# First attention of a two-layer transformer on one Trainium2 core: values and sums in one PSUM block of strips, the sums over four steps

## The reference, cut to what matters

```python
Q1, Q2 = Q[..., :dh], Q[..., dh:]                 # dh = 16
K1, K2 = K[..., :dh], K[..., dh:]
A1 = where(causal, Q1 @ K1.T * scaling, -inf)     # 2048 x 2048, and A2 likewise
attn = softmax(A1, -1) - lam * softmax(A2, -1)
O = attn @ V                                      # V: 2048 x 32
```

## Time and profile before

| | us |
|---|---|
| median of 3 runs | 4359.77 |
| lowest and highest run | 4359.03, 4366.46 |
| the profiled execution: its time | 4362.48 |
| the profiled execution: its span in the trace | 4360.6 |
| TensorE busy | 3700.6 (85% of the span) |
| VectorE busy | 2467.0 (57%) |
| ScalarE busy | 1754.4 (40%) |
| GpSimd busy | 1706.6 (39%) |

### The profile page before, as it was taken

How to read it: one execution, slowest core, us unless ns; L and a number is a source line. 1 busy time by engine, 2 the same in 40 slices (tenths; PEclk the granted TensorE clock), 3 DMA queues, 4 the chain that set the end, 5 groups by cost and what they waited for, 6 DMA issues and landing times. The chain is left out here.

```text
span 4360.6 us, 69689 instructions
## 1 busy us (share of the span) xinstructions
PE 3700.6 (85%) x21166; PEld 1647.8 (38%) x21231; DVE 2467.0 (57%) x4628; ACT 1754.4 (40%) x3522; POOL 1706.6 (39%) x1117
## 2 busy tenths in 40 slices
PE   6869999999999999999999996753899678896794
PEld 3322333232323232323233323642455445555462
DVE  4456766575757576767676753767211276666102
ACT  2324665666656566666666663110122141111110
POOL 1313555555555555555555554400344231110203
PEclk9978999999999999999999997855899899996897
DMA  4431111111111111111111103210443200001332
GB/s 156 154 120 33 34 37 33 34 35 35 35 35 35 35 35 35 35 36 34 38 33 38 31 9 96 82 40 0 121 91 76 45 24 4 0 0 39 111 111 87
DMA packets 202326, 224.92 MB, mean 52 GB/s; under 512 B 86673, under 2 KB 162706, under 8 KB 195858
## 3 DMA queue, kind: packets, MB, share of 16 engines
q1 hardware_dynamic: 186642, 195.39, 15.3%
q0 software_dynamic: 15360, 25.44, 3.1%
HBM read 139.12 MB, written 80.87 MB: 50 GB/s over the span
## 5 line engine op out<-in xcount | busy, mean ns | idle before, releaser
L638 POOL TENSOR_TENSOR attention_probs<-attention_probs 128x1024 f32<-128x1024 f32 (+2 forms) x640 | 1228.1, 1921 | 1160.2 <-PE attention_ps_o L791 1160.1
L708 DVE TENSOR_REDUCE attention_chunk_max<-attention_ps_m 128x1 f32<-128x512 f32 (+3 forms) x2560 | 1394.2, 604 | 457.4 <-PE attention_ps_m L823 280.6
L683 ACT ACTIVATE attention_probs<-attention_ps_s 128x512 f32<-128x512 f32 (+3 forms) x2560 | 1199.5, 532 | 826.9 <-PE attention_ps_s L772 459.7
L768 PE MATMUL attention_ps_s<-attention_q_stack,attention_k_stack 99*128 99x512 bf16 (+3 forms) x2560 | 821.6, 354 | 91.1 <-ACT attention_probs L683 70.1
L820 PE MATMUL attention_ps_m<-attention_k_stack,attention_q_stack 96*128 96x512 bf16 (+3 forms) x2560 | 772.5, 357 | 48.7 <-DMA attention_v_head<-v_rows 34.5
L791 PE MATMUL attention_ps_o<-attention_probs,attention_v_head 128*32 128x512 f32 (+3 forms) x5120 | 647.4, 558 | 8.6 <-issue 5.0
L768 PEld LDWEIGHTS attention_ps_s<-attention_q_stack,attention_k_stack 99*128 99x128 bf16 x2560 | 234.0, 98 | 668.4 <-ACT attention_probs L683 466.0
L820 PEld LDWEIGHTS attention_ps_m<-attention_k_stack,attention_q_stack 96*128 96x128 bf16 x2560 | 224.9, 97 | 628.7 <-DVE attention_chunk_max L708 490.2
L809 PE MATMUL attention_ps_l<-attention_probs,consts 128*32 128x512 f32 (+1 forms) x2560 | 352.6, 580 | 9.7 <-POOL attention_probs L638 1.0
L734 DVE TENSOR_TENSOR attention_out_sb<-attention_even_sb,attention_odd_sb 64x512 f32<-64x512 f32 x128 | 115.0, 898 | 296.8 <-ACT attention_even_sb L656 290.9
L823 PE MATMUL attention_ps_m<-mask_q_bf,ident_bf 128*128 128x128 bf16 x1024 | 225.5, 223 | 0.0
(11 more groups left out here) (283 smaller groups left out, 4108.8 us busy)
## 6 DMA issues: line engine op xcount, KB each, us to landing
qk_parts<-project_parts SPq DMA_DIRECT2D x64, 384.0 KB, 3.0
heads_out<-attention_out_sb SPq DMA_DIRECT2D x128, 128.0 KB, 2.3
out_heads<-heads_out SPq DMA_DIRECT2D x8, 2048.0 KB, 8.2
experts_w<-in_f_w SPq DMA_DIRECT2D x16, 1024.0 KB, 8.3
attention_q_stack<-qk_parts SPq DMA_DIRECT2D x32, 384.0 KB
attention_k_stack<-qk_parts SPq DMA_DIRECT2D x32, 384.0 KB
experts_w<-in_e_w SPq DMA_DIRECT2D x24, 512.0 KB, 4.8
v_rows<-project_v SPq DMA_DIRECT2D x8, 1024.0 KB, 4.2
```

Of the source, the lines that this page charges most:

```text
L638: pool.tensor_tensor(probs[:, to, :, lo:], probs[:, to, :, lo:], probs[:, k % RING_P, :, lo:], ALU.add).then_inc(pair_ok, 1)
L683: act.activation(probs[:, k % RING_P, a, left(k):], ps_s[(2 * k + a) % RING_S][:, left(k):], ACT.Exp, scale=float(DH) ** -0.5).then_inc(pr ...
L708: last = dve.tensor_reduce(chunk_max[:, a, jq, c:c + 1], ps_m[m % RING_M][:, 0:width(m)], AX.X, ALU.max)
L768: last = pe.matmul(psum[:, lo:], ks[at][0:WITH_MAX, a, kb * P:(kb + 1) * P], qs[at][0:WITH_MAX, a, tq * GROUP + lo:(tq + 1) * GROUP], star ...
```

## The change

What it does, part by part:

- **Values.** Four strips as before, but a strip is now (half of the queries, a), where the two "halves" are the even and the odd blocks of 128 queries of the tile. Every step makes up to four matmuls of 256 columns, and all steps of a turn sum into the same strips. ScalarE copies values and sums out with one instruction of 128 x 512, and nothing is left to add (L655, L656, L665 become one copy; L734 goes).
- **Sums.** They lie in the same PSUM bank beside the values: `ps_o` is now [128, 2, 2, 128], two buffers. GpSimd adds pairs of steps as before; VectorE adds the two pairs of a quad (`add_pairs`: two SBUF inputs, up to 128 x 1024 float32, in place), and TensorE takes one matmul of 256 columns per strip with ones for the whole quad.
- **Maxima.** The mask matmul L823 goes. On the diagonal, VectorE's reduction is replaced by `tensor_tensor_reduce`, which adds a float32 mask from SBUF (`mask_wide`), writes the sum back to PSUM and gives the maximum; its wait stands apart.
- **Order.** TensorE: score(k+2,0), first third of the items, score(k+2,1), second third, score(k+3,0), values(k), values(k+1), ones of the quad before when k%4 is 2, score(k+3,1), last third. VectorE: `add_pairs` of the quad before stands at the start of step k with k%4 = 2, ahead of that step's items. The ring `probs` has 10 steps.
- **Stores.** Four DMAs per turn in place of two. The next stage reads sums of 2 rows per head in place of 4.

```diff
-        RING_P, RING_S, RING_M, RING_O = 2 * QUAD, 3, 3, 2
+        RING_P, RING_S, RING_M, RING_O = 10, 3, 3, 2
...
-                    dve.wait_ge(max_ok, after * N_MAX + m + 1)
-                    last = dve.tensor_reduce(chunk_max[:, a, jq, c:c + 1], ps_m[m % RING_M][:, 0:width(m)], AX.X,
-                                             ALU.max)
+                    w, to = width(m), chunk_max[:, a, jq, c:c + 1]
+                    if c == jq // GT:
+                        wait_apart(dve, max_ok, after * N_MAX + m + 1, core.passed)
+                        last = dve.tensor_tensor_reduce(ps_m[m % RING_M][:, 0:w], ps_m[m % RING_M][:, 0:w],
+                                                        mask_wide[:, GROUP - w:], 1.0, -3.0e38, ALU.add, ALU.max, to)
+                    else:
+                        dve.wait_ge(max_ok, after * N_MAX + m + 1)
+                        last = dve.tensor_reduce(to, ps_m[m % RING_M][:, 0:w], AX.X, ALU.max)
...
+            def add_pairs(head, quad):
+
+                k = quad * QUAD
+                to, lo = k % RING_P, left(k + PAIR)
+                dve.wait_ge(pair_ok, head * PAIRS + (quad + 1) * 2)
+                dve.tensor_tensor(probs[:, to, :, lo:], probs[:, to, :, lo:], probs[:, (k + PAIR) % RING_P, :, lo:],
+                                  ALU.add).then_inc(quad_ok, 1)
...
                 for k in range(N_STEPS):
-                    ended = ends(k, 3)
-                    if head is not None and ended and not (ended[1] and is_first(head)):
-                        add_halves(head - 1 if ended[1] else head, ended[0])
-                    if after is not None:
-                        maxima(after, maxima_at(k, head is None))
+                    if at_head is not None and k % QUAD == 2:
+                        if k > QUAD:
+                            add_pairs(at_head.n, k // QUAD - 1)
+                        elif not is_first(at_head.n):
+                            add_pairs(at_head.n - 1, QUADS - 1)
+                    if next_head is not None:
+                        maxima(next_head.n, maxima_at(k, at_head is None))
...
-                for n in range(2):
-                    for a in range(2):
-                        strip, lo = (n * 2 + a) * DV, left(k + n)
-                        last = pe.matmul(ps_o[strip:strip + DV, lo:], vh[at][:, kb + n],
-                                         probs[:, (k + n) % RING_P, a, lo:], start=tq > 0 and kb == 0,
-                                         stop=kb == GT * (tq + 1) - 2, tile_position=(0, strip))
-                last.then_inc(values_ok, 2)
+                for strip, half, a, block in strips(k):
+                    last = pe.matmul(psum[strip:strip + DV, 0, block:], vh[at][:, kb], halves(k, a, half, block),
+                                     start=kb == 0, stop=False, tile_position=(0, strip), skip_group_check=True)
+                last.then_inc(values_ok, 1)
...
+                pe.wait_ge(quad_ok, head * QUADS + quad + 1)
+                for strip, half, a, block in strips(k):
+                    last = pe.matmul(psum[strip:strip + DV, 1, block:], core.c("ones")[:, 0:DV],
+                                     halves(k, a, half, block), start=False, stop=kb == GT * tq,
+                                     tile_position=(0, strip), skip_group_check=True)
                 last.then_inc(ones_ok, 1)
...
                     if more:
                         score(head, at, k + 2, 0)
+                        maxima(after, other, items[:third])
                         score(head, at, k + 2, 1)
-
-                    third = -(-len(items) // 3)
-                    maxima(after, other, items[:third])
-                    if more:
+                        maxima(after, other, items[third:2 * third])
                         score(head, at, k + 3, 0)
...
                     values(head, at, k)
-                    if not more and after is not None:
+                    values(head, at, k + 1)
+                    if k % QUAD == 2 and k > QUAD:
+                        ones(head, k // QUAD - 1)
+                    elif k == 2 and not is_first(head):
+                        ones(head - 1, QUADS - 1)
+                    if more:
+                        score(head, at, k + 3, 1)
+                    elif after is not None:
                         score(after, other, 0, 1)
                         score(after, other, 1, 0)
-                    maxima(after, other, items[third:2 * third])
-                    if more:
-                        score(head, at, k + 3, 1)
                     maxima(after, other, items[2 * third:])
-                    if k >= QUAD and k % QUAD == 0:
-                        ones(head, k // QUAD - 1)
-                    elif k == 0 and not is_first(head):
-                        ones(head - 1, QUADS - 1)
```

158 lines of the change are left out of this document (64 added, 94 removed).

## The result

| | before | after |
|---|---|---|
| median of 4 runs, us | 4359.40 | 5128.47 |
| lowest and highest run | 4355.14, 4366.46 | 5107.75, 5158.09 |
| ratio, 95% interval | | 1.177 [1.170, 1.183] |
| profiled execution: time, span | 4362.48, 4360.6 | 5140.85, 5138.6 |
| from head to head | 72.3 | 97.5 |

The account below looks back on a forecast made before the run. TensorE was taken as the bound, with little slack on VectorE. Per head, -6.7 saving + 21.4 stalls + 7.0 clock = +21.7 us, x 31 = +673, giving 5030 us (range 4700 to 5260).

Parts of the forecast that it names:

- TensorE's saving: Ones 5.8 and mask matmuls 1.9 us less, values 1.0 more: net 6.7 us per head less, if nothing else changes.
- stalls: TensorE waits for item reductions behind `add_pairs` at seven places per head: 18.6 us plus 2.8 in following iterations, 21.4.
- clock: TensorE's granted clock falls after idle times of 2.8 us, costing 1.0 us at each of seven stalls: 7.0 per head.
- the fourth item: Fourth open item after `add_pairs`, v being the end of the values: reached at v + 1.54, starts v + 4.4.
- Rival 2: VectorE's addition doesn't wait for GpSimd, or GpSimd is delayed in its place: +183, 4545 us; chance 0.08.
- The term of 2.8 for the following iteration: After each stall VectorE has a backlog, so the next iteration's fourth item comes 0.4 us too soon: 7 x 0.4.
- 18.6 us: Seven stalls per head ahead of the fourth item: five of 2.8 us and two of 2.3.
- rival 4: Value groups of 256 columns don't chain, each paying its fixed part and entry again: 4295 us; chance 0.02.
- Rival 3: TensorE stays the bound, without stalls, so the kernel gets faster: 4150 us; chance 0.07.
- Rival 1: Stalls as forecast, but TensorE's clock holds at full: +456, 4815 us; chance 0.25.
- `tensor_tensor_reduce` at no change: On the 32 diagonal items VectorE's masked reduction takes about as long as the one it replaces, 0.692 against 0.683 us.
- upper bound of 9: One more short vector instruction of 0.29 us per diagonal item: 9 us per head on VectorE, half shaded by the stalls.

Follow-up runs that it names:

- no_add: Changed kernel without VectorE's addition of the two pairs of a quad, so the sums miss every second pair: 4399.3 us, ratio 1.009.
- busy_stall: Changed kernel with eight more copies of a score matmul in each iteration with a stall, nothing left out: 4832.1 us, ratio 1.107.
- run 93: Not a run's label: the text says that in the whole run of the changed kernel, 93 narrow additions start under a GpSimd addition.
- one_input: Changed kernel with a reduction of one SBUF input in place of VectorE's addition, sums missing the second pairs: 4712.5 us, ratio 1.080.
- before_masked: Kernel before, with only the masked reduction on the diagonal items and no mask matmul; computes everything: 4331.7 us, ratio 0.992.
- mask_matmul: Changed kernel with the mask matmul and the plain reduction back in place of the masked reduction: 5020.6 us, ratio 1.152.
- ones_later: Changed kernel with VectorE's addition behind the first third of the items, ones one iteration later, ScalarE's copy two steps later: 4444.3 us, ratio 1.019.
- spread_ones_mask: Changed kernel with second third of items behind values and ones, addition behind first third, ones one iteration later, mask matmul back: 4453.1 us, ratio 1.019.
- spread: Changed kernel with the second third of the items back behind the values and ones, nothing left out: 4482.4 us, ratio 1.027.
- pair_ones: Changed kernel without VectorE's addition, TensorE taking ones of both pairs; second third of items behind values and ones, mask matmul back: 4463.0 us, ratio 1.022.

## Why the prediction was right, and where it wasn't

The ladder of periods gives each term its measured size: before 72.3, `no_add` 73.5, `busy_stall` 87.3, after 97.5.

| term, us per head | forecast | measured |
|---|---|---|
| TensorE's saving | -6.7 | +1.2 (no_add - before) |
| stalls | +21.4 | +13.8 (busy_stall - no_add) |
| clock | +7.0 | +10.2 (after - busy_stall) |
| sum | +21.7 | +25.2 |

The row of the stalls carries the addition's own time too, as the forecast's 2.8 us did. How exact the split between stalls and clock is, no run shows.

**The stall: right in its mechanism and in its times.** The forecast had the addition ending 0.54 (512 wide) or 1.08 (1024 wide) behind GpSimd's; it ended 0.55 and 1.09 behind. In the whole run 93 narrow and 126 wide ones start under a GpSimd addition; all end 546 to 554 or 1079 to 1089 ns behind it. It had the fourth item's place at v + 1.54 and its start at v + 4.4; they are v + 1.55 (1457.66, at k=14) and v + 4.33 (1471.15, at k=18). That one is the longest of the seven. `one_input` shows the wait: a reduction with one SBUF input passes beside GpSimd's addition, a `tensor_tensor` with two does not. The reduction also writes less to SBUF, but writing isn't what is held: L710 below writes to SBUF beside GpSimd, from one SBUF and one PSUM input, and keeps its 278 ns. Rival 2 falls with it, also in its second half: GpSimd's additions have their 1921 ns in both kernels. The Trainium skill, "SBUF — State Buffer", section "Who interferes with whom", says that a VectorE instruction with two SBUF inputs contends with a GpSimd instruction that reads SBUF, and that `tensor_reduce` never does; the trace agrees, with 1820 against 1208 ns in the same place.

**Missed in it:** the addition after a quad with diagonal steps is 512 wide, at k=6, 14 and 26, so 3 of the 7 stalls are 0.54 shorter (-1.6). With that, 18.6 us becomes 17.0; the seven stalls measure 16.0. The term of 2.8 for the following iteration wasn't there: at all other items TensorE waits 6.7 us per head in `busy_stall` and 7.1 in `no_add`. And the stalls don't all add to what was there: at the same seven places `no_add` already waits 2.6. The rest of the row is two things that nearly cancel: values and ones take 3.4 us per head more, mostly the ones' wait for the addition at k=34 (below), and the scores wait 2.9 less, as no wait for the DMAs of the maxima is left in `busy_stall`.

**The failed step: TensorE's saving.** The groups save what was costed (1.01 for the values pair, 0.42 for ones behind it), so rival 4 falls, and in the head without items the saving arrives: the last head takes 54.3 us in `no_add`, from its first score to its last ones, against 64.4 before (and 61.6 in `before_masked`, whose last head is the same code, so such a figure is good to some 3 us). The step was "6.7 us per head less, if nothing else changes", with "TensorE is the bound" ahead of it. TensorE wasn't the only bound. The forecast had read that VectorE has little slack in the iterations with items and that TensorE may run only three items ahead, but booked the saving as if neither mattered. What the runs show in its place: waits ahead of items of 9.7 us per head in place of 1.9, and a wait of 2.8 us at the head's end for the DMAs of the maxima. Why the items wait is argued, not shown: with strips of 1.0 to 1.4 us in which no item is issued, VectorE runs dry, and what it then has to do, TensorE waits for, three buffers later. That VectorE's share of this stretch is 0.82 before and 0.77 in `no_add` (its records merged, from a head's first item to its last) fits it: it is not full, yet waited for. The work taken from TensorE came back as waiting, and 1.2 us per head more. Rival 3 (4150 us) falls on the same fact: even with the addition taken out altogether the kernel is at 4399. This error (+7.9) and the oversized stalls (-7.6) nearly cancel, so that the total lies 98 us from the measured one is in good part luck.

**The clock: right in kind, undersized.** 10.2 in place of 7.0, but well within the bounds of 0 to 14. With idle times of 1.8 to 2.7 us, seven per head, it is 0.83 over the stage, and one is followed by 3.6 us of unbroken work at 0.53. Rival 1, the clock that holds, was set at 4815; `busy_stall`, which makes it hold, gives 4832. That they agree so closely is the same luck: its sum has -6.7 and +21.4, where +1.2 and +13.8 were measured.

**`tensor_tensor_reduce` at no change: wrong.** The duration was right (694 against 692), but the second instruction of 0.14 us was there, 4.5 us per head on VectorE, and 97.5 - 93.1 = 4.4 us of the period go with the masked form, although `mask_matmul` has the mask matmuls on TensorE again. Part of the 4.4 is the clock, 0.88 in place of 0.83. It is inside the forecast's upper bound of 9. The Trainium skill, "VectorE: DVE Perf Modes", section "Two Vector instructions with no wait between them", has an operation that also writes its accumulator as two instructions; the trace agrees, with 1024 records of 139 ns. The forecast cited it and gave it no weight. The same page's section "Rules for kernel authors" calls `tensor_reduce` the engine's slowest operation, which is not borne out here: 683 ns beside 694 for the masked form.

**Not foreseen: the maxima's chain at the end of a head.** Timeline of VectorE and TensorE, after:

```profile
1414.27 4.74 POOL L634 TENSOR_TENSOR attention_probs<-attention_probs 128x1024 f32<-128x1024 f32 x2 [0.47 <-PE attention_ps_o L785]
...
1415.04 0.28 DVE L710 TENSOR_TENSOR attention_max_rest<-attention_ps_m,attention_max_parts 32x128 f32<-32x128 f32 x1
...
1415.36 1.35 DVE L712 CAST attention_max_parts<-attention_max_rest 32x128 bf16<-32x128 f32 x1
...
1416.74 2.41 DVE L713 TENSOR_TENSOR attention_max_parts<-attention_max_rest,attention_max_parts 32x128 bf16<-32x128 f32 x1
1419.09 2.34 DVE L721 TENSOR_TENSOR attention_probs<-attention_probs 128x1024 f32<-128x1024 f32 x2
...
1420.34 1.08 PE L796 MATMUL attention_ps_o<-attention_probs,consts 128*32 128x256 f32 x8 [3.78 <-DVE attention_probs L721]
```

Two small instructions with 128 columns wait for GpSimd, the addition stands behind them, and the ones behind it: 3.8 us of TensorE once per head. Little of it shows in the period: the part of a head outside the items went from 18.1 to 20.0 us, measured from last to first item matmul. The same two instructions are as slow without the addition (means of 1333 and 2359 ns in `no_add`, against 264 and 280 before); there the DMAs that wait for them arrive late, and TensorE stands 2.8 us at the head's end. Where the second of them misses GpSimd's addition, in `ones_later` and `spread_ones_mask`, it has 280 ns again, and TensorE waits 19.8 and 3.7 us for these DMAs from 400 to 2580 us.

**Open.** `ones_later`, `spread` and the old mask together give nothing beyond `ones_later` alone: by the sums over the trace, waits ahead of items fall from 11.5 to 9.2 us per head, but the mask matmuls bring 1.7 back and waits ahead of strips another 0.8. Why 9.2 stay, and why TensorE pays in full in `pair_ones` while it still waits for items, no run here tells apart. No run has more than three buffers for the items, which would test the tie between the two engines directly.

## What to carry to other kernels

An instruction's price is read at its place in the queue: the same ten additions cost 729 us ahead of an iteration's items and some 110 behind a third of them, because of what another engine holds at that moment and who stands behind. And before a saving on the busiest engine is booked, ask how full its partner is in the same stretch and how many buffers tie the two; at 0.8 and three buffers here, nothing of 6.7 us arrived in a head with items.

## What the runs showed of the hardware

- A cast of 128 columns from SBUF to SBUF waits for GpSimd too, though it has one input. After (L712) it has a mean of 1373 ns and ends 0.08 us behind GpSimd's addition; before (L724) it also ends 0.08 behind, but starts only 0.18 ahead of that end and so has 265; the only one of a run that meets no addition takes 214. A `tensor_tensor` with one input in PSUM (L710) beside the same GpSimd addition stays at 278. The section of the Trainium skill named above counts casts among what can use both ports and then contend with GpSimd, and the trace agrees.
- The granted clock falls behind some single idle times of 1.8 to 2.7 us, and eight matmuls of 0.22 us placed in each keep it up: 8 x 7 x 0.22 = 12.3 us more work per head, and 296 us less for the kernel.
- Four strips of 256 float32 columns chained behind another such group cost 0.42 to 0.45 us each (`no_add`: 1.01 us for the pair of values less 0.56 for one group alone, and 0.42 for the ones behind it), with no visible price for the change of weights between values and ones.
